# Graph attention layer: scaled rows summed in fp32 instead of three bf16 parts, and scaled right behind the exponents

## What is computed

```python
h_trans = features @ Watt_w.T + Watt_b            # 12500 x 64
e_raw = sum(h_trans[dst] * tanh(h_trans[src] + e_r), -1)   # 212500 edges, sorted by dst
e_ij = leaky_relu(e_raw / 8)
exp_e = exp(e_ij - segment_max(e_ij, dst)[dst])
denom = segment_sum(exp_e, dst)
h_neigh = segment_sum(features[src] * exp_e, dst) / (denom + 1e-9)   # the division moved behind the sum
h_out = leaky_relu((x + h_neigh) @ W1.T + (x * h_neigh) @ W2.T + b1 + b2)
out = layernorm(x + h_out)
```

## Time and profile before

| | us |
|---|---|
| three runs | 2827.87, 2823.59, 2828.71 |
| median | 2827.87 |
| the profiled execution, its time | 2813.21 |
| its span (first to last instruction) | 2811.4 |
| DVE busy | 1652.8 (59%) |
| POOL busy | 1655.3 (59%) |
| ACT busy | 1602.6 (57%) |
| PE busy | 1365.9 (49%) |

### The profile page before, as it was taken

How to read it: one execution, slowest core, us unless ns; L and a number is a source line. 1 busy time by engine, 2 the same in 40 slices (tenths; PEclk the granted TensorE clock), 3 DMA queues, 4 the chain that set the end, 5 groups by cost and what they waited for, 6 DMA issues and landing times. The chain is left out here.

```text
span 2811.4 us, 32328 instructions
## 1 busy us (share of the span) xinstructions
PE 1365.9 (49%) x6440; PEld 1096.9 (39%) x6440; DVE 1652.8 (59%) x7936; ACT 1602.6 (57%) x2794; POOL 1655.3 (59%) x1670
## 2 busy tenths in 40 slices
PE   4344444455444444554445444554544555444455
PEld 4333343344333433443334334443433444333344
DVE  2256666655665656565666555655666556566567
ACT  2345555565555555565655556655555565656565
POOL 4466666666665666566666656666566666666660
PEclk7555555555555555555555555555555555555555
DMA  4333333333333333333333333333333333333331
GB/s 162 113 94 101 108 109 108 108 107 97 109 101 107 108 108 108 108 95 105 105 108 109 108 108 100 116 100 100 104 108 109 108 102 102 110 100 108 108 111 31
DMA packets 169270, 296.07 MB, mean 105 GB/s; under 512 B 111730, under 2 KB 111942, under 8 KB 169107
## 3 DMA queue, kind: packets, MB, share of 16 engines
q1 hardware_dynamic: 114689, 185.75, 19.9%
q0 software_dynamic: 53152, 107.98, 15.5%
q10 hardware_dynamic: 1266, 0.93, 0.1%
HBM read 284.43 MB, written 10.07 MB: 105 GB/s over the span
## 5 line engine op out<-in xcount | busy, mean ns | idle before, releaser
L628 POOL DMA_INDIRECT got<-table,src_i x1631 | 1625.7, 997 | 1074.5 <-DVE spare L1290 515.4
L949 PE MATMUL ps_hd<-hw,hotT 128*128 128x64 f32 x3322 | 731.9, 421 | 7.3 <-ACT hotT L735 7.3
L949 PEld LDWEIGHTS ps_hd<-hw,hotT 128*128 128x128 f32 x3322 | 721.9, 333 | 7.5 <-ACT hotT L735 7.5
L994 PE MATMUL ps_acc<-parts,hot 128*128 128x195 bf16 x1661 | 328.3, 364 | 637.9 <-DVE parts L1303 567.2
L750 ACT ACTIVATE edge<-edge 128x256 f32<-128x256 f32 (+1 forms) x444 | 176.6, 398 | 613.8 <-issue 499.8
L994 PEld LDWEIGHTS ps_acc<-parts,hot 128*128 128x128 bf16 x1661 | 208.8, 136 | 744.9 <-issue 619.8
L724 ACT ACTIVATE off<-dst_all,node 128x1024 bf16<-128x1024 int32 x222 | 424.7, 1913 | 121.3 <-remote 73.6
L1303 DVE TENSOR_TENSOR parts<-spare,parts 128x520 bf16<-128x520 f32 x222 | 147.1, 663 | 235.1 <-ACT parts L790 211.8
L1232 DVE CUSTOM_DVE_ANT_0 edge<-edge,ps_hd 128x64 f32<-128x64 f32 x1661 | 265.8, 217 | 18.8 <-remote 7.1
L1005 PE MATMUL ps_misc<-ident,sum_prod 128*128 128x128 f32 x111 | 52.4, 472 | 431.7 <-DVE sum_prod L1319 431.7
L735 ACT ACTIVATE hotT<-off,ones 128x1024 f32<-128x1024 bf16 x222 | 242.6, 1093 | 7.2
(11 more groups left out here) (137 smaller groups left out, 1974.1 us busy)
## 6 DMA issues: line engine op xcount, KB each, us to landing
dst_all<-in_dst SPq DMA_DIRECT2D x109, 960.5 KB
edge<-in_edge_attr SPq DMA_DIRECT2D x110, 480.0 KB
got<-table,src_i POOLq DMA_INDIRECT x1631
table<-hx SPq DMA_DIRECT2D x12, 512.0 KB
hw<-table SPq DMA_DIRECT2D x111, 32.0 KB
xw<-in_x SPq DMA_DIRECT2D x111, 32.0 KB
out<-y_out SPq DMA_DIRECT2D x111, 32.0 KB
x_piece<-in_x SPq DMA_DIRECT2D x3, 768.0 KB, 4.4
```

The costliest lines, as they stand in the source:

```text
L628: pool.indirect_dma_start(got[b.four][:, g, 0:2 * D], None, table, bass.IndirectOffsetOnAxis(ap=src_i[b.four][:, g:g + 1], axis=0))\
L949: last = pe.matmul(expanded(g, c), hotT[b.two][:, g, :], hw[b.two][:, :], start=True, stop=True)
L994: last = pe.matmul(a_parts, hot[b.four][:, g, :], parts[:, g, :, :].rearrange("p a d -> p (a d)"), start=(g == 0), stop=(g == tiles(b) - 1))
```

## The change

`rest` and the three bf16 parts go. `scale_rows` writes fp32 rows into one of two buffers, and PE sums them directly, 65 columns a tile, with a one-hot that is fp32 too. The one-hot has two buffers instead of four and is built in the step of its own block (behind `add(b, 1)`), not a step ahead. Of `place`, only the copy of `node` stays ahead of the exponents, as `set_node`. `scale_rows` follows `exponents` at once. `high_part`, `mid_part`, `left_part`, `low_part` are gone; ACT's `exp` of the carried weight becomes a call of its own. `numbers` gets a tile of its own. The order on SP, POOL and PE is not changed.

```diff
-        hot = [sb(f"hot{k}", [P, TILES, P], BF16) for k in range(BUFS)]
+        hot = [sb(f"hot{k}", [P, TILES, P]) for k in range(2)]
@@ ACT
-            def high_part(b, p):
-            def mid_part(b, p):
+            def carry_exponent(b):
+
+                act.wait_ge(consts, 5)
+                act.wait_ge(summed[NP - 1], b.n)
+                act.activation(carry_weight[:, :], carry_arg[:, :], ACT.Exp)
...
                 if exists(prev) and carried(prev):
+                    carry_exponent(prev)
                     copy_carry(before)
@@ PE sum_edges
-                pe.wait_ge(rest_low[p], b.n + 1)
+                pe.wait_ge(scaled[p], b.n + 1)
+                pe.wait_ge(hot_built[PIECE_CHUNKS[p][-1]], b.n + 1)
...
-                    last = pe.matmul(a_parts, hot[b.four][:, g, :], parts[:, g, :, :].rearrange("p a d -> p (a d)"),
+                    last = pe.matmul(a_sum, hot[b.two][:, g, :], rows[b.two][:, g, :],
@@ DVE
+            def set_node(b):
...
-                if c == 0 and follows(b, BUFS):
-
-                    dve.wait_ge(summed[NP - 1], b.n - (BUFS - 1))
+                if c == 0 and follows(b, 2):
+
+                    dve.wait_ge(consts, 5)
+                    dve.wait_ge(summed[NP - 1], b.n - 1)
...
-                dve.tensor_tensor(rest[:, a:z, :], got[b.four][:, a:z, D:2 * D + 1],
+                if follows(b, 2):
+
+                    dve.wait_ge(consts, 5)
+                    dve.wait_ge(summed[p], b.n - 1)
+                dve.tensor_tensor(rows[b.two][:, a:z, :], got[b.four][:, a:z, D:2 * D + 1],
...
-                    chain("sum", dve.tensor_reduce(sums[:, :], a_parts.rearrange("p (a d) -> p d a", a=3), AX.X, ALU.add), b)
+                chain("sum", dve.tensor_copy(sums[:, :], a_sum), b)
@@ DVE step
                 if exists(b):
                     add(b, 0)
+                if exists(nxt):
+                    set_node(nxt)
                 if exists(prev):
                     exponents(prev)
-                if exists(nxt):
-                    place(nxt)
-                    for c in range(NC):
-                        build_hot(nxt, c)
-                if exists(prev):
                     scale_rows(prev, 0)
                     scale_rows(prev, 1)
...
                     add(b, 1)
-                if exists(prev):
-                    left_part(prev, 0)
-                    left_part(prev, 1)
-                if exists(b):
+                    place(b)
+                    for c in range(NC):
+                        build_hot(b, c)
                     dot(b, 1)
                     add(b, 2)
-                if exists(prev):
-                    low_part(prev, 0)
-                if exists(prev):
-                    low_part(prev, 1)
-                if exists(b):
                     add(b, 3)
```

More of the change, by code:

```diff
@@ L210, in gnn_layer @@
         y_old = sb("y_old", [P, D])
-        rest = spare[:, 0:TILES * (D + 1)].rearrange("p (g d) -> p g d", d=D + 1)
+        rows = [spare[:, k * TILES * (D + 1):(k + 1) * TILES * (D + 1)].rearrange("p (g d) -> p g d", d=D + 1)
+                for k in range(2)]
         rows_i = spare[:, 0:SEARCH_ROW].bitcast(I32)
@@ L250, in gnn_layer @@
         row_iota = ps_row[:, 320:320 + P // 2].bitcast(BF16)
-        numbers = hot[0][:, 0, :]
         m_back = ps_misc[:, 0:2]
@@ L1095, in _ @@
                 dve.memset(got[k][:, :, 2 * D:2 * D + 1], 1.0).then_inc(ones_set, 1)
-            dve.tensor_scalar(numbers, ident[:, :], 0.0, number[:, 0:1], ALU.mult, ALU.add).then_inc(numbers_set, 1)
+            dve.tensor_scalar(numbers[:, :], ident[:, :], 0.0, number[:, 0:1], ALU.mult, ALU.add).then_inc(numbers_set, 1)
             dve.memset(gap[:, :], 0.0).then_inc(gap_set, 1)
@@ L1183, in chain @@
                 dve.wait_ge(own[name], b.n + 1)
-            def place(b):
-                dve.wait_ge(dst_in[b.four], (b.fours + 1) * 16)
-                if follows(b, 1):
-                    dve.wait_ge(hot_built[NC - 1], b.n)
+            def set_node(b):
                 if follows(b, 2):
@@ L1196, in place @@
                 dve.tensor_copy(node[b.two][:, :], column).then_inc(node_set, 1)
+            def place(b):
+                dve.wait_ge(dst_in[b.four], (b.fours + 1) * 16)
+                if follows(b, 1):
+                    dve.wait_ge(hot_built[NC - 1], b.n)
                 column = base_all[:, b.n:b.n + 1] if b.known else base_all[:, bass.ds(b.n, 1)]
@@ L1206, in build_hot @@
                 a, z = cols(b, c)
-                if c == 0 and follows(b, BUFS):
-                    dve.wait_ge(summed[NP - 1], b.n - (BUFS - 1))
+                if c == 0 and follows(b, 2):
+                    dve.wait_ge(consts, 5)
+                    dve.wait_ge(summed[NP - 1], b.n - 1)
                 dve.tensor_tensor(
-                    hot[b.four][:, a:z, :].rearrange("p g (n a) -> p g n a", a=2),
+                    hot[b.two][:, a:z, :].rearrange("p g (n a) -> p g n a", a=2),
                     row_iota.rearrange("p (z n a) -> p z n a", z=1, a=2).to_broadcast([P, z - a, P // 2, 2]),
@@ L1494, in general_block @@
             def general_block(b, k, i):
-                neighbours(b, node_rows(hx, b, D, 2 * D), in_parts=False)
+                neighbours(b, node_rows(hx, b, D, 2 * D))
                 add_bias(b)
```

54 lines of the change are left out of this document (7 added, 47 removed).

## The result

Where both kernels were first timed the changed kernel is slower: 3356.3 us, median of 3352.5 to 3362.1, against 2828.3 us; ratio 1.187, 95% interval 1.185 to 1.190. In the runs made to explain it this sign did not always hold. There the kernel before itself took either 2203 to 2205 us or 2768 to 2823 us, and beside 2203 us the changed kernel took 2142.4 us, ratio 0.972 (0.971 to 0.974).

What follows compares the result with a forecast made beforehand. Bound: a loop of burst (19.2 us), recovery, one-hot and scaling, 24.5 us a block. Pauses from 5.25 to 3.7 us, 105 times, save 163 us: 2650 profiled, 2665 us as run median; 8-in-10 range 2470 to 2900.

Steps and rivals of the forecast that it cites:

- hidden by the burst: TensorE (PE): its 18.2 us chain with the longer sums stays below the 19.2 us burst and costs nothing.
- the new pause of 3.7 us: POOL between bursts: pauses fall from 5.25 to 3.7 us, 105 times, 163 us saved.
- A long burst slows everybody, I take it as a fact.: Gather bursts on POOL: late in one, other engines' hand-offs are slow, and a pause cures it; cause not shown.
- Scaling leaves the loop, the index load is next.: DVE and POOL's release: 1.98 us between `dst_rel` and scaling leave the loop; block b+3's indices are late next.
- SP's list is not changed: SP's index load stays behind the load of x; pauses bound by it were 4.33 us on average.
- fp32 one-hot, 2.55 us: One-hot on DVE: 2.55 us a block in fp32 for 1920 columns, bounds 1.36 and 2.65.
- DVE's 4.75 us and ScalarE's copies go: Splitting removed: DVE loses 2.65 us of passes and 2.1 us of waiting for ACT; ACT loses four copies.
- Sums from 3.0 to 6.6 us: Sums on PE: two fp32 records a tile, 6.6 us a block instead of 3.0, bounds 3.0 and 6.6 + 0.3.
- PE takes it back: Rival: PE's hand-offs fall into the slow part, 18.2 + 6; no change, 2828 us; no-change chance 0.06.
- Burst on burst, slower: Rival: POOL runs on and the step crawls through a second burst; 3005 us, half as often 2915; chance 0.20.
- Port: Rival: `place` on DVE holds up gathers beside it through the shared port, 0.5 us a block, 2722 us; chance 0.04.

Runs made afterwards that it cites:

- the half sums: Changed kernel with 8 of each block's 15 sum matmuls, the others left out: 2141.0 us free; 2963.7 us held, against 2816.1 us for the kernel before.
- the bf16 variant: Changed kernel, order kept, rows scaled once into bf16 and one-hot in bf16: 2143.6 us free; 2954.6 us held, against 2786.9 us for the kernel before.

## Why the prediction was wrong

The forecast was 2665 us, the range 2470 to 2900, and slower had 0.21; the highest number in it was 3005. The step that failed is the cover over TensorE's longer sums, "hidden by the burst", and with it the new pause of 3.7 us, which came out at 11.1. In the terms of the sum: POOL's pauses went from 551 to 1178 us where 551 - 163 was forecast, its gathers from 1625.7 to 1544.1 us, together + 545 us, and the spans differ by 3360.3 - 2811.4 = 549. The steps in their own order:

- **"A long burst slows everybody, I take it as a fact."** Right for the trace it came from, wrong as a fact of the kernel: it comes and goes, and the sign of the result hangs on it. Nothing in one trace could show that.
- **Scaling leaves the loop, the index load is next.** Right: VectorE idles for 0.28 us ahead of scaling, for `prob`, and the indices release POOL 101 times. **"SP's list is not changed", pause 3.7 us.** Wrong: 11.1 us. The step looked at the place of the index load in the list and not at what is queued ahead of it: the store of the block three before, which waits for VectorE's last operation behind the scan. When the scan slid from the middle of the burst to 3 us behind its end, store, indices and POOL slid with it. Moving the load away gave back only 156 us, so this is a link of the chain and not its cause.
- **fp32 one-hot, 2.55 us.** Measured 260.2 / 111 = 2.34 us, inside the bounds. No cost of it shows in either condition (the half sums, where it is whole).
- **DVE's 4.75 us and ScalarE's copies go.** Gone, as said. In the held condition the four passes are worth 0.7%, in the free one all of the 2.8%.
- **Sums from 3.0 to 6.6 us, "hidden by the burst".** The size was right, 766.6 / 111 = 6.9 us, the upper bound. The cover is what failed. The step set a chain of 18.2 us, at normal hand-offs, against a burst of 19.2 us, in the same text that said hand-offs late in a burst are not normal. In the free condition the cover is there (2141.0 us with half the sums, 2142.4 with all). In the held one it covers half of the stream, and the other half costs about 380 us: the hand-off from the rows to the scan alone, taken as a part of 3.5 us, took 8.67 us in the step shown. The rival "PE takes it back" named this, but put only 6 us on the chain and found no change.
- **Burst on burst, slower.** The only rival on the right side, but its mechanism is not in the changed kernel: behind the start-up all its bursts are those of a single block. It is in the bf16 variant, with 12 joined pairs at 28.2 us a block where the rival said 26.2. That the whole fp32 stream keeps the bursts apart by making the scaling late is how I read it; no run shows it.
- **Port.** It had 0.04 and the wrong place (`place`). Gathers lengthened by VectorE beside them are all of the gain in the free condition, in the other direction: passes that go away. The earlier trace rows held the evidence, gathers of 997 ns on average against the 0.94 to 0.95 us of a single one in the earlier trace rows.

What stays open: what the held condition is; why the whole fp32 stream brings the hand-off to the scan to the very end of the hold and half of it doesn't (theory one has the effect, not its cause); whether instructions or semaphores are late; and whether a pace slower than 1.43 us a gather would let the changed kernel run through. No kernel here beats both: the changed one is ahead in the free condition, the kernel before in the held one.

## What to carry to other kernels

Before a verdict on a few per cent, time the kernel before again beside the new one on more than one occasion: here the ratio was 0.972 or 1.187 for the same two programs. Where POOL's own gathers set the pace, look at which VectorE passes run beside them, since their cost stands in the gathers' mean time and not in any wait. And when a cover is claimed for longer work on one engine, the cover has to be counted with the hand-offs as slow as the trace shows them at that place, and with everything that is queued ahead of the next release.

## What the runs showed of the hardware

In some executions, late in a burst of indirect gathers and behind it, the other engines start microseconds after what they waited for is done; in others they don't (kernel before 2203 us or 2768 to 2828 us, changed kernel 2142 or 3356 us; chip 9 showed both, 2203 and 2787 us for the kernel before). The longest of these holds end about 21.46 us behind the start of a burst of 15 gathers and 42.59 us behind that of 30, and 21.5 to 22 us at a slower pace of 1.36 us a gather. In the same place of a burst (13 to 14 us into it) the same hand-off takes 0.04 us in one kernel and 7.7 to 8.0 us in another, so that neither the place nor the gathers alone decide. The gathers themselves are not slower then: 997 ns on average in the kernel before when held, 1003 when free, and in the changed kernel their data, by the transfer records, is all in 19.7 us behind the burst's start, 1.3 us behind the last gather. Slowing POOL from 1.25 to 1.36 us a gather went with a loss of 140 us instead of 528 us. Gathers beside VectorE passes with an fp32 and a bf16 input took 1.18 and 1.21 us instead of 0.94. A gather of 64 rows takes 924 ns where one of 128 takes 965.
